# A fused two-block GNN kernel: block 1 projects x that is centred but not yet scaled, and the leaky ReLU moves ahead of the mask

## The chip, the cores and the metric

The kernel runs on one core of one Trainium2 chip. The metric is the device time of one execution in microseconds; times are medians of three runs. The engines are TensorE (PE, matrix products), VectorE (DVE), ScalarE (ACT), GpSimd (POOL) and SyncE (SP, which issues loads). Each works through its own instructions in order and waits on semaphores that the others raise.

## The reference

256 nodes with 768 features, 4096 edges sorted by destination, self-loops added. Two graph attention networks, each behind a residual and a layer norm without gain:

```python
x = layernorm(x + L0(x))     # L0: gat_conv, 8 heads of 768, elu, gat_conv, 1 head of 768
x = layernorm(x + L1(x))     # L1: below; layernorm(v) = (v - mean) / sqrt(var + 1e-5)

# L1, with h0 = its input
h = gat_conv(h0, W1, a_src1, a_dst1, b1)          # 4 heads of 256
h = relu(layer_norm(h) * g1 + be1) + (h0 @ Wr1 + br1)
o = gat_conv(h, W2, a_src2, a_dst2, b2)           # 1 head of 768
out = layer_norm(o) * g2 + be2 + (h @ Wr2 + br2)

# gat_conv, for each head
xl = x @ W
e  = leaky_relu(a_src . xl[src] + a_dst . xl[dst], 0.2)
alpha = exp(e - max over the node's edges) / sum over the node's edges
out[dst] += alpha * xl[src]
```

## The kernel before

Nodes are two tiles of 128 rows (i = 0, 1). The edge list is turned into a dense 256 x 256 matrix of counts, so that a softmax over a node's edges is one over a row, with `far` (-1e30) where there is no edge. Every product is made in three passes, with each operand split into a rounded high part and a low part: ACT rounds (`..._hi`), POOL or DVE subtracts (`..._lo`), PE sums hi x hi, hi x lo and lo x hi. Nothing is scheduled by a tool: each engine's order is written out by hand.

**Weights.** SP loads them into `raw`, ACT rounds each chunk of 128 rows (`split_hi`, in block 1 `chunks_hi`, L373), POOL subtracts it (`split_lo`, in block 1 `chunks_lo`, L380), PE takes it when POOL's count says so. In block 1 there are 24 chunks of 128x512, numbered in this order: W1's first half (0 to 5, `w1a`), its second half (6 to 11, `w1b`), Wr1's halves (12 to 17 and 18 to 23), then 16 chunks of 128x768 for W2 and Wr2. Nine slots of a ring hold the wide chunks, so the rounding of chunk 9 and later ones waits until PE has used chunk 0 and later ones for tile 1. PE's order in block 1 is: transposes of x, w1a for tile 0, w1a for tile 1, w1b for tile 0 (with the scores of heads 0 and 1 ahead of chunk 8), w1b for tile 1, Wr1.

**Block 0** (`A_CONV2` is the index of its second convolution) takes one head per turn of a loop. A head's chain is: dot products of the features with both attention vectors (DVE, L1402), the source dots spread over all columns by PE (`scores`, L968), masking with a running maximum (`masked_scores`, L1457, DVE), four operations of 2 to 4 columns that make two biases, two exponentials per tile on ACT (L746 and L747, since exp of a leaky ReLU is the larger of two exponentials), DVE's maximum of the two and product with the counts (L1477 and L1481, or L1509 and L1511), then the transposes of the weights and PE's aggregation.

**Between the blocks** DVE adds x to the convolution's result (`y_piece`, L1655), takes mean and variance (`y_stats`), POOL takes the inverse root (`inverse_root`, L629 and L632), DVE applies both (`x1`, L1666), PE transposes (`transpose_x1`, L1186), ACT rounds, DVE subtracts, PE projects (`wide_product`, L1202). Dummy products (`keep_warm`, L934) fill PE's gaps. POOL's part of this stretch is

```python
chunks_lo(wide[:6])
for i in range(NT):
    inverse_root(0, i)
chunks_lo(wide[6:9])

pool.wait_ge(rows_loaded, 16 * 8)
pool.tensor_tensor(rows_d[:, 2, :], rows_d[:, 2, :], rows_d[:, 3, :], ALU.add).then_inc(be_added, 1)
pool.wait_ge(be_added, 1)
pool.wait_ge(x1_done, NT)
for i in range(NT):
    pool.tensor_tensor(shift(i), x_sb[:, i, :], rows_d[:, 2, :], ALU.add).then_inc(shifted, 1)
chunks_lo(wide[9:])
```

with the two additions L651 and L655. `shift` is x plus constants, wanted only for the output.

**In block 1** the bias of the residual product is laid into PSUM by PE ahead of it (`residual_bias`, L1217).

Of the kernel before, what the change touches and what calls it, by code (L numbers as in the profile page):

```python
# [117 lines left out]
def build_gnn(nc, x, src, dst, b0_W1, b0_as1, b0_ad1, b0_b1, b0_W2, b0_as2, b0_ad2, b0_b2,  # L118
# [5 lines left out]
    with ctx:  # L124
# [42 lines left out]
        cap1 = sb("cap1", [P, PAIRS])  # L167
        cap2 = sb("cap2", [P, PAIRS])
        bias1 = sb("bias1", [P, PAIRS])
        bias2 = sb("bias2", [P, PAIRS])  # L170
# [6 lines left out]
        rstd = sb("rstd", [P, NT])  # L177
        partial = sb("partial", [P, 2])
# [29 lines left out]
        NAT_AT = [6 * BANK, 0]  # L208
# [3 lines left out]
        TOP1_AT = 7 * BANK  # L212
        X1T_AT = [3 * BANK, 5 * BANK]
# [4 lines left out]
        TOP_AT = T_AT + N  # L218
# [46 lines left out]
        cap_done = sem("cap_done")  # L265
        e_done = sem("e_done")
        e_max_done = sem("e_max_done")
# [7 lines left out]
        bias_done = sem("bias_done")  # L275
# [35 lines left out]
        x1_done = sem("x1_done")  # L311
        tile0_done = sem("tile0_done")
# [145 lines left out]
        def tops(a):  # L458
            at = TOP1_AT + 2 * first_head(a) if is_gat1(a) else ACC if a is FIRST_HEAD else TOP_AT
            return ps[:, at:at + NT * heads_of(a)]  # L460

        def small(a):
            return slice(2 * first_head(a), 2 * (first_head(a) + heads_of(a)))

# [3 lines left out]
        def x1T_part(t, i, part):  # L468

            k0, k1 = 0 if part == 0 else X1T_PARTS[0], X1T_PARTS[part]  # L470
            at = X1T_AT[i] + k0 * P
            return (t[:, k0:k1, i * P:(i + 1) * P],
                    ps[:, at:at + (k1 - k0) * P].rearrange("p (k n) -> p k n", n=P))
# [19 lines left out]
        ON_ACT = [(3, 0)]  # L493

# [92 lines left out]
        def _(pool):  # L587
# [35 lines left out]
            def inverse_root(n, i):  # L623
# [8 lines left out]
                pool.tensor_tensor(rstd[:, i:i + 1], ve[:, i:i + 1], half[:, :], ALU.pow).then_inc(rstd_done, 1)  # L632
# [33 lines left out]
        def _(act):  # L666
# [56 lines left out]
            def features_hi(a, tiles=range(NT)):  # L723
                for i in tiles:
                    if a == A_GAT2:
                        act.wait_ge(b2_added, i + 1)
                    else:
                        act.wait_ge(a_dst_done, before(a) + HH * (i + 1))
                    act.activation(feat(h_hi, a, i), source_at(a, i), ACT.Copy).then_inc(h_hi_done, 1)
# [8 lines left out]

            def exps(a, order):

                act.wait_ge(bias_done, 2 * a + 2)
                for i in order:
                    for k in range(first_head(a), first_head(a) + heads_of(a)):
                        c = 2 * k + i
                        at = masked_at(a, k - first_head(a), i)
                        act.activation(e1[:, k, i, :], at, ACT.Exp, bias=bias1[:, c:c + 1]).then_inc(e_done, 1)  # L746
                        act.activation(at, at, ACT.Exp, bias=bias2[:, c:c + 1], scale=SLOPE).then_inc(e_done, 1)  # L747
# [44 lines left out]
            def softmax_and_elu(h, last=False):  # L792
                projected_hi(h)
# [23 lines left out]
            projected_hi(0)  # L817
            att_for(1)

            act.wait_ge(counted, NT)  # L820
            act.activation(ramp_sum, ps[:, COUNT_AT[0]:COUNT_AT[0] + NT * N], ACT.Copy).then_inc(ramps_copied, 1)
            for c in (0, 1, 2):
                split_hi(act, 2, c)
            exps(0, (1, 0))
            split_hi(act, 2, 3)
# [25 lines left out]
            act.wait_ge(a_dst_done, before(A_CONV2) + 2)  # L851
# [5 lines left out]
            chunks_hi(3, 9)  # L857
            for i in range(NT):
# [15 lines left out]
            for half_at, v in ((0, b1_as2), (1, b1_ad2)):  # L874
                act.dma_start(att[:, half_at * D:(half_at + 1) * D], v[0:1, :].partition_broadcast(P))\
                   .then_inc(att_loaded, 16)
            exps(A_GAT1B, (0, 1))
            chunks_hi(21, 24)
            weights_hi(A_GAT1B)
            chunks_hi(24, 27)  # L880

# [4 lines left out]
            h1_hi(0, 0)  # L886
            chunks_hi(27, 30)
# [7 lines left out]
            chunks_hi(36, 39)  # L895
            features_hi(A_GAT2, tiles=(1,))
# [6 lines left out]
        def _(pe):  # L903
# [205 lines left out]
            for c in range(CH):  # L1109
                if c == 2:  # L1110
                    pe.wait_ge(b1_ready, 2)
                    count_edges(0, COUNT_HALF)
                    count_loops()
                    count_edges(COUNT_HALF, ET)
                if c == 3:
                    scores(0)
# [74 lines left out]
            keep_warm(4, idle)  # L1191

            def wide_product(q, at, i, biased=False, passes=ALL):
# [4 lines left out]
                for n, (a, b) in enumerate(three(node_tile(xT_hi, k, i), node_tile(xT_lo, k, i),  # L1198
# [3 lines left out]
                    last = pe.matmul(ps[:, to:to + HW], a, b, start=k == 0 and n == 0 and not biased,  # L1202
# [5 lines left out]
            def residual_bias(part):  # L1208

                if part == 0:  # L1210
                    pe.wait_ge(pick_set, 3)
                    pe.wait_ge(bias_row_done, 2)
                else:
                    pe.wait_ge(bias_done, 2 * A_GAT1B + 2)
                for i in range(NT):
                    to = 4 * BANK + i * HC + part * HW
                    pe.matmul(ps[:, to:to + HW], bias_pick[0:BIAS_ROWS, :], bias_rows[part],  # L1217
                              start=True, stop=False, skip_group_check=True)
# [22 lines left out]
            transpose_x1(1)  # L1241
            for i in range(NT):
                for q in w1a[2:] if i == 0 else w1a:
                    if q["k"] == X1T_PARTS[0] or i == 1 and q["k"] == 0:
# [27 lines left out]
            residual_bias(0)  # L1272
            for i in range(NT):
                for q in wr1a:
# [6 lines left out]
                    last = wide_product(q, 4 * BANK, i, biased=True)  # L1281
                if i == 0:
                    last.then_inc(r_done, 1)
# [10 lines left out]
            residual_bias(1)  # L1294
            for i in range(NT):
                for q in wr1b:
                    if i == 0 and q["k"] == 3:
                        aggregate_half(A_GAT1B)
                    if i == 1 and q["k"] == 2:
                        transpose_h1(0, 0)  # L1300
                    last = wide_product(q, 4 * BANK, i, biased=True)
                if i == 0:
                    last.then_inc(r_done, 1)
# [5 lines left out]
            for q in w2[:H1_PART]:  # L1309
                if q["k"] == 2:  # L1310
                    transpose_h1(0, 1)
                w2_product(q, 0)
# [34 lines left out]
        def _(dve):  # L1347
# [42 lines left out]

            def dots(a, t, half_at, done, tiles=range(NT)):
# [4 lines left out]
                for i in tiles:  # L1396
# [3 lines left out]
                    for k in range(first_head(a), first_head(a) + n):  # L1400
# [4 lines left out]
                                                 1.0 - SLOPE if half_at else 1.0, 0.0,  # L1405
# [40 lines left out]
            def masked_scores(a):  # L1446

                n = heads_of(a)
                top = tops(a)
                if not in_block0(a):  # L1450
                    dve.wait_ge(scores_bc, a + 1)
                if is_gat1(a):
                    dve.wait_ge(h_lo1_done, 2 * late(a) + 2)
                for k in range(n):
                    for i in range(NT):
                        at = s_at(a, k)
                        dve.tensor_tensor_reduce(masked_at(a, k, i), ps[:, at:at + N], far[:, i, :], 1.0, -3.0e38,  # L1457
                                                 ALU.add, ALU.max, top[:, 2 * k + i:2 * k + i + 1])\
                           .then_inc(masked, 1)
                upto = before(a) + 2 * n  # L1460
                dve.wait_ge(masked, upto)
                dve.wait_ge(a_dst_done, upto)
                d, of = a_d[:, small(a)], small(a)
# [415 lines left out]
```

## Time and profile before

| | |
|---|---|
| median of 3 runs (lowest, highest) | 373.2 us (372.81, 374.55) |
| the profiled execution's own time | 373.22 us |
| its span, first to last instruction | 371.1 us |
| mean granted TensorE clock | 0.998 of full speed |
| busy: PE, PE's weight loads, DVE, ACT, POOL | 355.4, 304.1, 219.4, 213.7, 247.6 us |

The profile is one execution. A row of a timeline gives start, duration, engine, line, operation, output and inputs, shapes, and how many equal instructions are merged; in brackets how long the engine had been idle and what ended it. Starts are counted from the span's start. The ends of matrix products are modelled, so their starts are the better mark: a product of 512 columns starts every 0.228 us.

### The profile page before, as it was taken

To read this page: it belongs to the slowest core of one execution; us is meant where nothing else is said; L and a number is where in the kernel's file an instruction comes from. 1 tells how busy PE (TensorE), PEld (TensorE's weight loads), DVE (VectorE), ACT (ScalarE), POOL (GpSimd) and SP (SyncE) were. 2 spreads that over 40 slices of the span, in tenths; PEclk is the share of its full clock that TensorE was granted. 3 is DMA by queue.
4 is the path that set the end of the run, shared out by engine and by line. 5 is a ranking of instruction groups with operands and counts; after the bars stand their busy time and mean duration, and the time that the engine had idled before them with its cause. 6 is when DMAs were issued, how large, how long until landed. Compare 5 with 4: busy or idle time off the path is not lost.

```text
span 371.1 us, 6198 instructions
## 1 busy us (share of the span) xinstructions
PE 355.4 (96%) x2104; PEld 304.1 (82%) x2104; DVE 219.4 (59%) x570; ACT 213.7 (58%) x373; POOL 247.6 (67%) x170
## 2 busy tenths in 40 slices
PE   7899979999999999999999999998988999999994
PEld 4788868888988988898898898897666788888883
DVE  3996766428328345543741923736776788763875
ACT  4996466756755664673765665565352667244601
POOL 2789619595866947849668595692268976397911
PEclk9999999999999999999999999999999999999999
DMA  7979936637637536754663752755073256436002
GB/s 250 320 244 262 389 128 197 224 95 250 178 96 257 184 134 180 241 172 126 215 239 98 251 174 91 241 188 204 0 219 134 90 165 193 165 94 242 8 0 85
DMA packets 24544, 65.15 MB, mean 176 GB/s; under 512 B 1952, under 2 KB 3024, under 8 KB 24528
## 3 DMA queue, kind: packets, MB, share of 16 engines
q1 hardware_dynamic: 20720, 55.19, 44.7%
q10 hardware_dynamic: 3808, 9.76, 8.8%
q8 instruction: 9, 0.15, 0.2%
q14 instruction: 7, 0.06, 0.0%
HBM read 64.15 MB, written 0.79 MB: 175 GB/s over the span
## 4 chain that ended last, share of the span: by engine, by line
PE 71%; ACT 7%; DVE 6%; issue 6%; POOL 5%; DMA 4%; SPq 0%; POOLq 0%; DVEq 0%; ACTq 0%
PE ps L918 52%; PE ps L1202 7%; PE ps L1003 6%; DMA raw<-in_L_gnn_W 4%; POOL ring_lo L364 3%; ACT ring_hi L351 2%; PE ps L982 1%; PE ps L1268 1%; PE ps L1036 1%; ACT rows_hc L689 1%; POOL ring_lo L380 1%; ACT z L689 1%; PE ps L968 1%; ACT am L689 1%; POOL x_sb L619 1%
## 5 line engine op out<-in xcount | busy, mean ns | idle before, releaser
L364 POOL TENSOR_TENSOR ring_lo<-raw,ring_hi 128x768 fp32r<-128x768 f32 x94 | 170.7, 1851 | 75.1 <-ACT ring_hi L351 75.0
L351 ACT ACTIVATE ring_hi<-raw 128x768 fp32r<-128x768 f32 x96 | 77.5, 851 | 35.2 <-PE ps L918 28.6
L380 POOL TENSOR_TENSOR ring_lo<-raw,ring_hi 128x512 fp32r<-128x512 f32 (+1 forms) x40 | 59.7, 1521 | 24.0 <-ACT ring_hi L373 23.9
L1402 DVE CUSTOM_DVE_ANT_0 e<-ps,att 128x768 f32<-128x768 f32 (+1 forms) x54 | 40.0, 796 | 51.3 <-PE ps L918 48.7
L918 PE MATMUL ps<-ring_hi,zT_hi 128*128 128x512 f32 (+1 forms) x256 | 69.4, 346 | 0.9 <-DVE zT_lo L1558 0.6
L918 PE MATMUL ps<-ring_lo,zT_hi 128*128 128x512 f32 (+1 forms) x256 | 67.4, 338 | 0.0
L918 PE MATMUL ps<-ring_hi,zT_lo 128*128 128x512 f32 (+1 forms) x256 | 67.2, 338 | 0.0
L918 PE MATMUL ps<-ring_hi,xT_hi 128*128 128x512 f32 x192 | 51.3, 343 | 2.3 <-POOL ring_lo L364 1.0
L918 PE MATMUL ps<-ring_lo,xT_hi 128*128 128x512 f32 x192 | 50.3, 339 | 0.0
L918 PE MATMUL ps<-ring_hi,xT_lo 128*128 128x512 f32 x192 | 50.2, 338 | 0.0
L918 PEld LDWEIGHTS ps<-ring_hi,zT_lo 128*128 128x128 f32 x256 | 43.2, 188 | 5.6
L918 PEld LDWEIGHTS ps<-ring_lo,zT_hi 128*128 128x128 f32 x256 | 43.1, 188 | 5.6
L918 PEld LDWEIGHTS ps<-ring_hi,zT_hi 128*128 128x128 f32 x256 | 42.0, 189 | 6.6 <-DVE zT_lo L1558 0.9
L1549 DVE SCALAR_TENSOR_TENSOR ps<-ps,b_plus,z 128x256 f32<-128x256 f32 x48 | 21.2, 487 | 29.2 <-ACT z L776 29.2
L918 PEld LDWEIGHTS ps<-ring_hi,xT_hi 128*128 128x128 f32 x192 | 32.3, 188 | 7.4 <-issue 1.5
L373 ACT ACTIVATE ring_hi<-raw 128x512 fp32r<-128x512 f32 (+1 forms) x40 | 26.6, 722 | 17.9 <-PE ps L918 10.0
L918 PEld LDWEIGHTS ps<-ring_hi,xT_lo 128*128 128x128 f32 x192 | 32.8, 188 | 4.2
L918 PEld LDWEIGHTS ps<-ring_lo,xT_hi 128*128 128x128 f32 x192 | 32.8, 188 | 4.1
L721 ACT ACTIVATE h_hi<-ps 128x768 fp32r<-128x768 f32 x18 | 13.7, 809 | 22.4 <-DVE a_d L1402 20.8
L1003 PE MATMUL ps<-pT_hi,h_hi 128*128 128x256 f32 x96 | 26.2, 284 | 0.3 <-ACT pT_hi L753 0.3
L1003 PE MATMUL ps<-pT_hi,h_lo 128*128 128x256 f32 x96 | 26.1, 283 | 0.0
L1558 DVE SCALAR_TENSOR_TENSOR zT_lo<-ps,zT_hi 128x512 fp32r<-128x512 f32 x24 | 16.6, 692 | 15.9 <-ACT zT_hi L782 15.9
(163 smaller groups left out, 562.2 us busy)
## 6 DMA issues: line engine op xcount, KB each, us to landing
raw<-in_L_gnn_W SPq DMA_DIRECT2D x54, 768.0 KB, 4.4
raw<-in_L_gnn_Wr SPq DMA_DIRECT2D x8, 768.0 KB, 4.3
att<-in_L_gnn_a_src ACTq DMA_DIRECT2D x10, 384.0 KB, 4.6
att<-in_L_gnn_a_dst ACTq DMA_DIRECT2D x10, 384.0 KB, 5.4
raw<-in_L_gnn_W SPq DMA_DIRECT2D x4, 384.0 KB, 6.1
x_sb<-in_x SPq DMA_DIRECT2D x3, 256.0 KB, 5.7
rows_hc<-in_L_gnn_b SPq DMA_DIRECT2D x1, 512.0 KB, 6.3
rows_hc<-in_L_gnn_g SPq DMA_DIRECT2D x1, 512.0 KB, 7.2
```

The lines of the kernel that those rows point to most:

```text
L351: eng.activation(slot_hi(c), raw_chunk(c), ACT.Copy).then_inc(hi_done, 1)
L364: eng.tensor_tensor(slot_lo(c), raw_chunk(c), slot_hi(c).bitcast(F32), ALU.subtract)\
L373: eng.activation(ring_hi[:, q["ring_at"]:q["ring_at"] + w], raw[:, q["raw_group"], q["raw_at"]:q["raw_at"] + w], ACT.Copy)\
L380: eng.tensor_tensor(ring_lo[:, q["ring_at"]:q["ring_at"] + w], raw[:, q["raw_group"], q["raw_at"]:q["raw_at"] + w], ring_hi[:, q["ring_at" ...
L689: act.activation(ramp(t), iota[:, :], ACT.Relu, bias=bias).then_inc(ramp_act_done, 1)
L721: act.activation(feat(h_hi, h, i), source_at(h, i), ACT.Copy).then_inc(h_hi_done, 1)
L918: last = pe.matmul(ps[:, at + to:at + to + hi - lo], a, b[:, lo:hi], start=start and n == 0 and to != D, stop=stop and n == PASSES - 1, sk ...
L1003: return pe.matmul(ps[:, at:at + N], feat(features, 0, j)[:, ch:ch + P], weights_part[:, 0, j, :], start=first, stop=final, skip_group_che ...
L1202: last = pe.matmul(ps[:, to:to + HW], a, b, start=k == 0 and n == 0 and not biased, stop=k == KD - 1 and n == PASSES - 1, skip_group_check ...
L1402: dve.tensor_tensor_reduce(junk[:, at:at + w], of[:, (k - first_head(a)) * w:(k - first_head(a) + 1) * w], att[:, half_at * row + k * w:ha ...
L1549: dve.scalar_tensor_tensor(ps[:, at:at + N], ps[:, at:at + N], b1_plus[:, bass.ds(KD * h + t, 1)], z[:, t * N:(t + 1) * N], ALU.add, ALU.m ...
L1558: dve.scalar_tensor_tensor(zT_lo[:, 2 * q:2 * q + 2, :].rearrange("p k n -> p (k n)"), ps[:, at:at + 2 * N], -1.0, hi.bitcast(F32), ALU.ad ...
```

## The change

It has two parts.

1. In every softmax the leaky ReLU is formed first. ACT forms 0.2 x (source dot) - 0.8 x (destination dot) (`leaks`, the destination dots now come multiplied by -0.8), DVE takes the maximum with the source dot (`leaky_scores`), then masks it, negated, with a running minimum (`tile_tops`), and ACT takes one exponential with that minimum as its bias. The four small operations and the second exponential go. In block 0's heads the low part of the features of one tile stands on each side of `tile_tops`.
2. Between the blocks, x is centred in PSUM's and ACT's passes with a mean from running sums, and goes to the transposes without the root. The root is taken meanwhile and put on the dot products, on the features (`scale` of ACT's rounding, one factor in DVE's subtraction) and, by four new ACT passes (`residual_scale`), on Wr1's product, behind which the bias is now added. x itself is scaled by ACT (`x1_scale`), which raises `x1_done`. The ten dummy products behind the aggregation go, and two stay of four behind the transposes.

POOL's code is not touched but for the root's name. The core of the diff:

```diff
+            def leaks(a):
+
+                act.wait_ge(scores_bc, a + 1)
+                for i in range(NT):
+                    act.wait_ge(a_dst_done, before(a) + heads_of(a) * (i + 1))
+                    for k in range(heads_of(a)):
+                        at = s_at(a, k)
+                        act.activation(e1[:, first_head(a) + k, i, :], ps[:, at:at + N], ACT.Identity,
+                                       bias=a_d[:, pair(a, k, i)], scale=SLOPE).then_inc(leak_done, 1)
...
+                for n, i in enumerate(order):
+                    act.wait_ge(masked, before(a) + heads_of(a) * (n + 1))
+                    for k in range(heads_of(a)):
+                        at = masked_at(a, k, i)
+                        act.activation(at, at, ACT.Exp, bias=top[:, pair(a, k, i)], scale=-1.0).then_inc(e_done, 1)
...
             def softmax_and_elu(h, last=False):
+                leaks(h)
                 projected_hi(h)
                 exps(h, (1, 0))
...
-            act.wait_ge(a_dst_done, before(A_CONV2) + 2)
+            leaks(A_CONV2)
             projected_tile_hi(A_CONV2, 1)
...
-            chunks_hi(3, 9)
-            for i in range(NT):
...
+            def centre_wide(i):
+
+                lo, hi = NAT_PIECES[0]
+                act.wait_ge(mean_done, i + 1)
+                act.activation(x_sb[:, i, lo:hi], ps[:, NAT_AT[i] + lo:NAT_AT[i] + hi], ACT.Identity,
+                               bias=minus_mean[:, i:i + 1]).then_inc(wide_centred, 1)
...
+            def x1_scale(i):
+
+                act.wait_ge(x1T_ps, 2 * i + 2)
+                act.wait_ge(rstd_done, i + 1)
+                act.activation(x_sb[:, i, :], x_sb[:, i, :], ACT.Copy, scale=rstd0[:, i:i + 1]).then_inc(x1_done, 1)
+
+            def residual_scale(part, i):
+
+                if i == 0:
+                    act.wait_ge(r_product, part + 1)
+                else:
+                    act.wait_ge(chunk_used, plan[(3 + part) * KD - 1]["n"] + 1)
+                of = ps[:, 4 * BANK + i * HC + part * HW:4 * BANK + i * HC + (part + 1) * HW]
+                act.activation(of, of, ACT.Copy, scale=rstd0[:, i:i + 1]).then_inc(r_scaled, 1)
+
+            chunks_hi(3, 6)
+            centre_wide(0)
+            chunks_hi(6, 7)
+            x1_hi(0)
+            centre_wide(1)
+            chunks_hi(7, 9)
+            x1_hi(1)
+            x1_scale(0)
+
             features_hi(A_GAT1A, tiles=(0,))
             chunks_hi(9, 14)
+            x1_scale(1)
             features_hi(A_GAT1A, tiles=(1,))
             chunks_hi(14, 15)
+            leaks(A_GAT1A)
             exps(A_GAT1A, (0, 1))
...
-            idle = WT_AT[0]
-            keep_warm(10, idle)
 
             def transpose_x1(i):
 
-                pe.wait_ge(x1_done, i + 1)
+                pe.wait_ge(wide_centred, i + 1)
                 for k in range(KD):
-                    at = X1T_AT[i] + k * P
+                    if k == X1T_PARTS[0]:
+                        pe.wait_ge(rest_centred, i + 1)
...
             transpose_x1(0)
-            keep_warm(4, idle)
...
+            keep_warm(2, PROJ)
...
+                    if i == 0 and q["k"] == 5:
+                        residual_bias(0, 0)
+                        residual_bias(0, 1)
...
             def softmax(h):
-                masked_scores(h)
-                projected_lo(h)
+                leaky_scores(h)
+                dve.wait_ge(leaky_done, 2 * h + 2)
+                projected_lo(h, 0)
+                for i in (1, 0):
+                    tile_tops(h, i)
+                projected_lo(h, 1)
                 normalised(h)
                 weights_lo(h)
...
             y_piece(0, 0)
             y_piece(0, 1)
-            y_stats(0)
+            y_centre(0)
             y_piece(1, 0)
-            x1(0)
             y_piece(1, 1)
-            y_stats(1)
+            y_centre(1)
             x1_lo(0, 0)
             x1_lo(0, 1)
-            x1(1)
+            y_stats(0)
+            y_stats(1)
             x1_lo(1, 0)
             x1_lo(1, 1)
```

How the instructions stand on the engines. On PE, from the dummies behind the aggregation to the first projection's second pair of chunks, before (`x_sb` is x, `ring` the weights, `xT` the transposed x):

```order
L934 MATMUL ps<-zeros 128x512 x10
L1186 MATMUL ps<-ident,x_sb 128x128 [waits x1_done]
L1186 MATMUL ps<-ident,x_sb 128x128 x5
L934 MATMUL ps<-zeros 128x512 x4
L1202 MATMUL ps<-ring_hi,xT_hi 128x512 [waits lo_pool,x1T_hi_done]
...
L1202 MATMUL ps<-ring_hi,xT_lo 128x512 [waits lo_pool]
L1186 MATMUL ps<-ident,x_sb 128x128 [waits x1_done]
L1186 MATMUL ps<-ident,x_sb 128x128 x5
```

and now:

```order
L1245 MATMUL ps<-ident,x_sb 128x128 [waits wide_centred]
L1245 MATMUL ps<-ident,x_sb 128x128 x3
L1245 MATMUL ps<-ident,x_sb 128x128 [waits rest_centred]
L1245 MATMUL ps<-ident,x_sb 128x128
L994 MATMUL ps<-zeros 128x512 x2
L1261 MATMUL ps<-ring_hi,xT_hi 128x512 [waits lo_pool,x1T_hi_done]
```

The ten dummies are gone and the transposes wait for the centring. Those of tile 1 now stand four chunks into the projection, where two stood before.

On ACT, from the rounding of tile 1's transposes to the features of tile 1, before (`h_hi` are block 1's features):

```order
L861 ACTIVATE xT_hi<-ps 128x2x128 [waits x1T_ps]
L729 ACTIVATE h_hi<-ps 128x512 [waits a_dst_done]
L373 ACTIVATE ring_hi<-raw 128x512 [waits chunk_used,raw_full0]
L373 ACTIVATE ring_hi<-raw 128x512 [waits chunk_used] x2
L373 ACTIVATE ring_hi<-raw 128x512 [waits chunk_used,raw_full1]
L373 ACTIVATE ring_hi<-raw 128x512 [waits chunk_used]
L729 ACTIVATE h_hi<-ps 128x512 [waits a_dst_done]
```

and now:

```order
L889 ACTIVATE xT_hi<-ps 128x2x128 [waits x1T_ps]
L895 ACTIVATE x_sb<-x_sb,rstd 128x768 [waits rstd_done,x1T_ps]
L737 ACTIVATE h_hi<-ps,rstd 128x512 [waits a_dst_done]
L378 ACTIVATE ring_hi<-raw 128x512 [waits chunk_used,raw_full0]
L378 ACTIVATE ring_hi<-raw 128x512 [waits chunk_used] x2
L378 ACTIVATE ring_hi<-raw 128x512 [waits chunk_used,raw_full1]
L378 ACTIVATE ring_hi<-raw 128x512 [waits chunk_used]
L895 ACTIVATE x_sb<-x_sb,rstd 128x768 [waits rstd_done,x1T_ps]
L737 ACTIVATE h_hi<-ps,rstd 128x512 [waits a_dst_done]
```

The scaling of x is new on ACT: tile 0's ahead of the first features, tile 1's behind the five chunks that follow them.

On POOL the rows of this stretch stand as before, now with these lines:

```order
L385 TENSOR_TENSOR ring_lo<-raw,ring_hi 128x512 [waits hi_done] x3
L658 TENSOR_TENSOR rows_d<-rows_d 128x768 [waits rows_loaded]
L662 TENSOR_TENSOR am<-x_sb,rows_d 128x768 [waits x1_done,be_added]
L662 TENSOR_TENSOR am<-x_sb,rows_d 128x768
L385 TENSOR_TENSOR ring_lo<-raw,ring_hi 128x512 [waits hi_done] x15
```

Nothing moved here; `x1_done` is raised by ACT's L895 and no longer by DVE.

## Rows read from the trace of the kernel before

**Rows 1.** The page, part 1: engine, busy us, share of the span, instructions.

```profile
PE 355.4 (96%) x2104; PEld 304.1 (82%) x2104; DVE 219.4 (59%) x570; ACT 213.7 (58%) x373; POOL 247.6 (67%) x170
```

**Rows 2.** The list of waits, PE: us in total, times, longest.

```profile
PE ps L1186 <- DVE x_sb L1666: 1.0, 1, 1.0
...
PE ps L1290 <- DVE z L1735: 0.2, 1, 0.2
```

**Rows 3.** The timeline, PE, from the aggregation to w1a's last product for tile 0.

```profile
275.39 2.33 PE L934 MATMUL ps<-zeros 128*128 128x512 bf16 x10
277.73 0.87 PE L1186 MATMUL ps<-ident,x_sb 128*128 128x128 f32 x6
...
279.12 0.58 PE L1202 MATMUL ps<-ring_hi,xT_hi 128*128 128x512 f32 x1
...
281.86 0.88 PE L1186 MATMUL ps<-ident,x_sb 128*128 128x128 f32 x6 [1.00 <-DVE x_sb L1666]
...
285.09 0.39 PE L1202 MATMUL ps<-ring_hi,xT_lo 128*128 128x512 f32 x1
```

**Rows 4.** The timeline, POOL and DVE's second x1, 280 to 298.

```profile
280.11 4.08 POOL L380 TENSOR_TENSOR ring_lo<-raw,ring_hi 128x512 fp32r<-128x512 f32 x3
280.18 1.63 DVE L1666 TENSOR_SCALAR x_sb<-z,mv,rstd 128x768 f32<-128x768 f32 x1
...
284.15 1.84 POOL L651 TENSOR_TENSOR rows_d<-rows_d 128x768 f32<-128x768 f32 x1
...
286.07 3.66 POOL L655 TENSOR_TENSOR am<-x_sb,rows_d 128x768 f32<-128x768 f32 x2
...
289.68 7.57 POOL L380 TENSOR_TENSOR ring_lo<-raw,ring_hi 128x512 fp32r<-128x512 f32 x6
```

**Rows 5.** The timeline, PE's weight load ahead of w1b's chunk 11, tile 0.

```profile
293.54 0.19 PEld L1202 LDWEIGHTS ps<-ring_hi,xT_hi 128*128 128x128 f32 x1 [0.47 <-POOL ring_lo L380]
```

**Rows 6.** The timeline of one head of block 0's loop, all engines.

```profile
207.31 1.51 ACT L721 ACTIVATE h_hi<-ps 128x768 fp32r<-128x768 f32 x2 [2.79 <-DVE a_d L1402]
...
212.63 0.88 DVE L1516 TENSOR_SCALAR am<-ps,rz 128x256 f32<-128x256 f32 x2
...
214.28 0.60 PE L982 MATMUL ps<-ident,am 128*128 128x128 f32 x4
```

**Rows 7.** The timeline of A_CONV2's softmax, all engines.

```profile
266.97 0.43 DVE L1457 CUSTOM_DVE_ANT_0 ps<-ps,far 128x256 f32<-128x256 f32 x1 [0.18 <-PE ps L968]
...
268.31 0.47 ACT L746 ACTIVATE e<-ps,bias 128x256 f32<-128x256 f32 x1 [0.68 <-DVE bias L1468]
...
268.68 0.44 ACT L747 ACTIVATE ps<-ps,bias 128x256 f32<-128x256 f32 x1
...
269.62 0.42 DVE L1481 SCALAR_TENSOR_TENSOR e<-ps,counts 128x256 f32<-128x256 f32 x1
...
270.11 0.44 PE L994 MATMUL ps<-ident,e 128*128 128x128 f32 x2 [0.59 <-DVE e L1481]
...
271.12 0.48 PE L1036 MATMUL ps<-h_hi,pT_hi 128*128 128x512 f32 x1
```

**Rows 8.** The timeline, DVE's first dots of block 1 and ACT behind them.

```profile
285.63 0.42 DVE L1402 CUSTOM_DVE_ANT_0 e<-ps,att 128x256 f32<-128x256 f32 x1 [1.43 <-PE ps L1202]
...
287.13 0.60 ACT L729 ACTIVATE h_hi<-ps 128x512 fp32r<-128x512 f32 x1 [3.71 <-DVE a_d L1402]
...
287.63 2.71 ACT L373 ACTIVATE ring_hi<-raw 128x512 fp32r<-128x512 f32 x5
```

**Rows 9.** Groups by line and shape, ACT: busy us, mean ns, idle before.

```profile
L351 ACT ACTIVATE ring_hi<-raw 128x768 fp32r<-128x768 f32 x96 | 77.5, 851 | 35.2 <-PE ps L918 28.6 <-DMA raw<-in_L_gnn_W 6.6
...
L734 ACT ACTIVATE x_sb<-z,offset,rstd 128x768 f32<-128x768 f32 x1 | 1.0, 1028 | 12.6 <-POOL offset L635 12.6
```

**Rows 10.** The timeline, PE, the bias products ahead of Wr1's first half.

```profile
298.56 0.73 PE L1217 MATMUL ps<-zT_hi,bias_pick 33*128 33x512 f32 x2
```

**Rows 11.** The timeline, PE, the dummies at the kernel's start.

```profile
1.34 3.58 PE L934 MATMUL ps<-zeros 128*128 128x512 bf16 x8 [1.34 <-POOL zeros L589]
```

More of the change, by code:

```diff
@@ L886, in _ @@
             h1_hi(0, 0)
+            residual_scale(1, 1)
             chunks_hi(27, 30)
@@ L1201, in wide_product @@
                         continue
-                    last = pe.matmul(ps[:, to:to + HW], a, b, start=k == 0 and n == 0 and not biased,
+                    last = pe.matmul(ps[:, to:to + HW], a, b, start=k == 0 and n == 0,
                                      stop=k == KD - 1 and n == PASSES - 1, skip_group_check=True)
@@ L1206, in wide_product, with residual_bias @@
                 return last
[L1208 to L1218, printed above, removed]
+            def residual_bias(part, i):
+                pe.wait_ge(pick_set, 3)
+                pe.wait_ge(bias_row_done, 2)
+                pe.wait_ge(r_scaled, R_ORDER.index((part, i)) + 1)
+                to = 4 * BANK + i * HC + part * HW
+                pe.matmul(ps[:, to:to + HW], bias_pick[0:BIAS_ROWS, :], bias_rows[part],
+                          start=False, stop=True, skip_group_check=True).then_inc(r_done, 1)
             def narrow_product(q, at, i, tile, **more):
@@ new lines, in leaky_scores, with tile_tops @@
+                dve.wait_ge(leak_done, before(a) + NT * n)
+                for i in range(NT):
+                    for k in range(n):
+                        at = s_at(a, k)
+                        dve.tensor_tensor(masked_at(a, k, i), ps[:, at:at + N], e1[:, first_head(a) + k, i, :], ALU.max)\
+                           .then_inc(leaky_done, 1)
+            def tile_tops(a, i):
+                n = heads_of(a)
+                for k in range(n):
+                    if isinstance(a, int):
+                        dve.wait_ge(leaky_done, before(a) + n * i + k + 1)
+                    at = masked_at(a, k, i)
+                    dve.tensor_tensor_reduce(at, at, far[:, i, :], -1.0, 3.0e38, ALU.add, ALU.min, top[:, pair(a, k, i)])\
+                       .then_inc(masked, 1)
@@ L1478, in weigh @@
-                for k in range(n):
-                    c = 2 * (g + k) + i
-                    dve.wait_ge(e_max_done, before(a) + n * i + k + 1)
-                    dve.scalar_tensor_tensor(e2[:, g + k, i, :], masked_at(a, k, i), 1.0, counts[:, i, :],
-                                             ALU.mult, ALU.mult, accum_out=zsum[:, c:c + 1]).then_inc(p_done, 1)
-            def dots0(h):
-                dve.wait_ge(att_loaded, 32 * (h + 1))
-                dots(h, a_s, 0, a_src_done)
-                dots(h, a_d, 1, a_dst_done, tiles=(0,))
-                dve.wait_ge(scores_bc, h + 1)
-                dots(h, a_d, 1, a_dst_done, tiles=(1,))
@@ L1562, in _ @@
             both_dots(0)
-            projected_lo(0)
+            for i in range(NT):
+                projected_lo(0, i)
+            dve.wait_ge(h_lo0_done, NT)
+            leaky_scores(0)
             bank = ps[:, COUNT_AT[0]:COUNT_AT[0] + NT * N].rearrange("p (i n) -> p i n", n=N)
@@ L1642, in _ @@
             inverse_sums(A_CONV2)
-            y = [z[:, i * D:(i + 1) * D] for i in range(NT)]
             dve.wait_ge(xb_done, NT)
@@ L1804, in _ @@
                .then_inc(eps_done, 1)
+            y = [z[:, i * D:(i + 1) * D] for i in range(NT)]
             nat = [ps[:, GAT2_NAT_AT[i]:GAT2_NAT_AT[i] + D] for i in range(NT)]
```

188 lines of the change are left out of this document (98 added, 90 removed).

## The prediction

> **What bounds the kernel now.** I read the page first: TensorE (PE) is busy for 355.4 us, 96% of the span [rows 1], so only work or waits that stand in PE's own stream can move the end. Then the list of waits: all of PE's together are small, and the one that the change aims at, the wait of the transposes (L1186) for the normalised x (L1666), is 1.0 us [rows 2]. Then PE's timeline between the aggregation of block 0's second convolution and block 1's first projection: ten dummy products fill 275.39 to 277.73, six transposes of x's tile 0 follow, four more dummies, the first projection at 279.12, and the transposes of tile 1 wait until 281.86; the last product of the first projection's tile 0 starts at 285.09 [rows 3]. The dummies count as busy but do nothing, so some 3 to 4 us of this stretch could be saved. Last, GpSimd's timeline (POOL) of the same stretch [rows 4] and PE's row at 293.54 [rows 5]: three chunks of W1's second half are subtracted on POOL behind the two additions L655, and PE waits for the last of them. POOL delivers chunk 11 at 289.68 + 3 x 1.26 = 293.46 and PE takes it at 293.54. Here POOL, not PE, sets the time.
>
> **The new softmax.** In every softmax two exponentials per tile, two maxima behind them and four small operations become two ScalarE (ACT) reads, two maxima ahead of the masking, and one exponential per tile. In block 0's heads PE never waits for it. Before, the last of VectorE's (DVE) normalising ends at 212.63 + 0.88 = 213.51 and PE transposes at 214.28, a slack of 0.77 [rows 6]. After: the last dot product ends just ahead of ACT's start at 207.31 [rows 6], so the second ACT read runs from 207.33 to 207.80, maxima 207.83, h_hi done 209.20, h_lo tile 0 from 209.23 (0.87 to the next), two maskings of 0.35, h_lo tile 1, two products with the counts, sums and normalising: end 213.64. The slack is 0.64: cost 0 in the six heads of the loop, for as long as this cover holds; beyond it each 0.1 us costs 0.6 in all. Heads 0 and 1 lose nothing that lasts.
>
> At A_CONV2 the chain is bare. Before: DVE masks PE's scores at 266.97, its product with the counts starts at 269.62 for tile 0, PE's transposes at 270.11, the aggregation at 271.12 [rows 7]. After, DVE first waits for two ACT reads (0.37 from start to start, 0.47 long, as the exponentials in [rows 7]), to 267.83, then runs one maximum more ahead of the weights and the four small operations (0.5) less: the product of tile 0 starts at 270.10 instead of 269.62, tile 1 is where it was, and ACT's copy lets the aggregation start 0.35 later. **Term 1: +0.35.**
>
> **The shorter front.** The transposes of tile 0 wait for centred x, not for the root. DVE's sum and mean end near 274.6, ACT's centring (0.6) near 275.25; PE is through with the aggregation at 275.39 + 0.35 = 275.74, so they start there instead of at 277.73. From them to the first projection it is 1.39 as before (277.13); then 1.12 + 0.46 for the two chunks, 1.37 for two more, 0.63 for tile 1's transposes, which find their data centred by 277.9, and 1.22 up to the last product's start: 281.93 for the former 285.09. **Term 2 (with term 1 inside): PE is 3.16 early** at this point. Bounds: 2.6 if mean and centring take 0.5 longer, 3.5 if the softmax costs nothing.
>
> **What is late next.** POOL's order is untouched: chunks 0 to 5, two roots, chunks 6 to 8, the addition L651, a wait for both tiles of normalised x, the two L655 (3.61 from start to end), and only then chunk 9 [rows 4]. But x is now normalised by ACT (x1_scale), and the one of tile 1 stands behind features_hi of tile 0 and behind five chunks. Before, DVE met the wait at 280.18 + 1.63 = 281.81 and POOL came to it at 286.07 [rows 4]. After:
> - the roots: DVE's statistics now stand behind tile 0's low parts, tile 1's are ready at 280.6, the root takes 0.9 more, and chunk 6 starts at 281.47 instead of 280.11; with the 5.96 from there to L655 POOL reaches the wait at 287.4;
> - DVE's dots start 0.54 after PE's last product, as before (285.09 to 285.63): 282.47; ACT's features start 1.50 later, the five chunks 0.50 after that and last 2.71 with the last start 0.1 earlier than their end [rows 8]: to 287.2. the last of them, chunk 13, must also wait until PE has used W1's fifth chunk for tile 1, at 282.16 + 15 x 0.228 and some 0.3 for the result to land, 285.9, which it has;
> - x1_scale of tile 1: a 768-wide ACT pass is 0.85 plain and 1.03 with two operands per partition [rows 9]; with one I take 0.93: done near 288.2.
> So L655 starts at 288.2 instead of 286.07, chunk 9 is there at 291.8 + 1.26 = 293.1, chunk 11 at 295.6. PE wants chunk 9 at 281.93 + 0.23 + 27 x 0.228 + 0.44 = 288.75 and stands for 4.3 us. It takes chunk 11 at 295.65 for the former 293.54. **Term 3: all of term 2 is gone, and PE is 2.1 late.** How early PE came to the stall doesn't matter; only ACT's chain does. Bounds: L655 can't start before W1's fifth chunk is used for tile 1 (285.9), one ACT chunk (0.54) and the scaling (0.85) later, 287.3, which makes it 1.2 late; if each link of ACT's chain takes 0.1 to 0.2 more it is 2.9.
>
> **Behind it.** Four bias products move: two pairs in front of Wr1's halves (0.73 a pair [rows 10]) become one pair and two singles, with a change of operands around each; the trace shows no single one, so between 0 (the same work) and 0.7 (a pair's 0.73 for each single), and I take the nearer end, 0.2. The waits that they bring (for four ACT scalings of Wr1's product) are met: by ACT's order each scaling is done before PE comes to its bias product, the third by only some 0.3. PE's wait of 0.25 for DVE at L1290 [rows 2] is filled by them: -0.2. No wait of PE for block 1's scores or weights is in the list before, and PE now comes later to them; the last softmax loses its four small operations and gains the read, and PE's wide products cover it. **Term 4: 0** (-0.2 to +0.5).
>
> **Sum.** 2.1 + 0 on the profiled execution's own 373.22 us (371.1 of span and 2.1 around it), which is the median of the three runs, 373.2: **375.3 us**, 0.56% slower. About 0.5% (1.87 us, so beyond 375.07 or 371.33) is what a measurement of this kernel tells from no change.
>
> **Rivals.**
> 1. *The stall also costs the clock* (28%). PE has nothing to do for 4.3 us at 288.75 and is half idle until 295.65. In this trace PE never stands so long after the start: dummies fill such gaps, and the granted clock stays at its upper level, 2.4 GHz (0.998 in the mean). What half of it costs shows at the start: there eight dummies take 3.58 us (0.448 each) [rows 11], and ten take 2.33 (0.233) in [rows 3]. At half speed chunks 9 to 11 take 1.3 each and end 0.6 later, and what is left of some 3.6 us of slow running falls on tile 1's products: 0.6 to 2.1 more, 1.3 as the middle: **376.6**. Against it: 4.3 us may be too short for the clock to fall. The Trainium skill, TensorE: Matmul & The Clock Gate, "HAM oscillation", says that an array left idle between bursts goes back to the lower clock and begins the next burst cold; by that, this rival would be the forecast. No stretch of this trace shows such a wait, so it stays a rival.
> 2. *Less is lost* (10%). If ACT's chain runs ahead and L655 starts at 287.3 (the lower bound), PE is 1.2 late: **374.4**, not to be told from no change.
> 3. *The front's gain survives* (6%): the other side. It needs POOL to deliver chunk 9 before PE asks for it, so L655 to begin before 283.8, or POOL to be quick enough to catch up. It then ends at 373.2 - 3.2 + 0.2 = **370.2**. It decides at an L655 start of 284.2: earlier is faster by 0.5%, and at 286.07 there is no change. For it speaks that PE really has the 3.16; against it that POOL itself can't be at L655 before 285.3 and that x1_scale stands where it stands.
> 4. *The heads lose their cover* (6%). If ACT's two reads come 0.2 later than the 0.64 of slack allows, six heads lose 1.2: 376.5.
>
> **Chances.** My forecast (POOL late by 1.6 to 2.6, clock kept: 374.8 to 376.0, of which 60% lie above 375.07) has 50%. Slower by over 0.5%: 0.30 + 0.27 (rival 1) + 0.06 (rival 4) = 0.63. Within 0.5%: 0.20 + 0.01 + 0.09 = 0.30; the rest of rival 2 and rival 3 make faster 0.07. The range: rivals 1 and 4 reach to 377.4, rival 2's upper half to 374.1; what lies below holds about 0.12, above 0.06.
>
> **What would show it.** In the trace of after: PE's transposes of x at about 275.7 with no wait before tile 1's; the last product of tile 0 at 281.9; L655's successor on POOL starting at 288.2 with a wait for ACT's scaling ahead; a wait of PE for POOL of about 4.3 us, the longest of all, near 289, and two of 0.6 behind it; chunk 11 used at 295.65; the heads of block 0 with PE's period unchanged. The granted clock behind 293 tells forecast from rival 1. I'd be wrong if the scaling on ACT came before the five chunks in time, if POOL's wait were met by 286, or if block 0's heads grew.

## The result, and the profile after

The changed kernel takes 377.5 us in the median of 9 runs (376.03 to 378.76), the kernel before in 9 runs beside it 372.81 us (372.23 to 374.55): a ratio of 1.0123, 95% interval 1.010 to 1.0146. It is slower, as forecast (375.3), and 0.1 us above the range (374.1 to 377.4). A second set of 6 runs gave 377.5 again.

The profiled execution took 378.57 us, with a span of 376.7 us, 5.6 us more than the kernel before. Some 2 us of these arise in the first 11 us, where TensorE's rate differs from run to run in either kernel (last section). The heads of block 0, whose softmax is new, add nothing: from the start-up's 16 products with `am` (26.06 in the kernel before, 28.05 here) to PE's scores of block 0's second convolution it is 240.46 us there and 240.40 here. So positions are compared behind these scores, a mark that all kernels have. They start at 266.52 in the kernel before and at 268.45 here, 1.93 later, each behind the same wait of 0.68. **From this mark to the end of the span the kernel before takes 104.58 us and the changed one 108.25: 3.67 more.** "On before's scale" below means 1.93 less. Of the kernel before, the timeline, PE, has the mark and the last product of w1b:

```profile
266.52 0.40 PE L968 MATMUL ps<-ident,a_s 128*128 128x128 f32 x2 [0.68 <-DVE a_s L1624]
...
298.23 0.40 PE L1202 MATMUL ps<-ring_hi,xT_lo 128*128 128x512 f32 x1
```

The page of the changed kernel, parts 1 and 2, against [rows 1]: PE is busy longer for fewer instructions, and the row of the granted clock has one slice at 6.

```profile
PE 357.5 (95%) x2092; PEld 306.0 (81%) x2092; DVE 213.3 (57%) x529; ACT 221.0 (59%) x382; POOL 247.3 (66%) x170
...
PEclk9999999999999999999999999999999699999999
```

The list of waits of the changed kernel, PE (us in total, times, longest), against [rows 2]: the wait for normalised x and the 0.2 us at the transposes of h1 are gone, and one of 4.3 us for POOL is there.

```profile
PE ps L1261 <- POOL ring_lo L385: 4.3, 1, 4.3
```

The timeline of the changed kernel, PE, from the second convolution to the end of the slow stretch, against [rows 3]:

```profile
268.45 0.40 PE L1028 MATMUL ps<-ident,a_s 128*128 128x128 f32 x2 [0.68 <-DVE a_s L1683]
...
273.51 0.47 PE L1096 MATMUL ps<-h_hi,pT_hi 128*128 128x512 f32 x1 [0.22 <-ACT pT_hi L775]
...
277.77 0.82 PE L1245 MATMUL ps<-ident,x_sb 128*128 128x128 f32 x6
278.43 0.59 PE L994 MATMUL ps<-zeros 128*128 128x512 bf16 x2
279.06 0.50 PE L1261 MATMUL ps<-ring_hi,xT_hi 128*128 128x512 f32 x1
...
283.77 0.40 PE L1261 MATMUL ps<-ring_hi,xT_lo 128*128 128x512 f32 x1
...
290.50 0.39 PE L1261 MATMUL ps<-ring_hi,xT_lo 128*128 128x512 f32 x1
295.19 0.79 PE L1261 MATMUL ps<-ring_hi,xT_hi 128*128 128x512 f32 x1 [4.31 <-POOL ring_lo L385]
295.79 0.63 PE L1261 MATMUL ps<-ring_lo,xT_hi 128*128 128x512 f32 x1
296.21 0.63 PE L1261 MATMUL ps<-ring_hi,xT_lo 128*128 128x512 f32 x1
...
300.48 0.44 PE L1261 MATMUL ps<-ring_hi,xT_hi 128*128 128x512 f32 x1
300.75 0.39 PE L1261 MATMUL ps<-ring_lo,xT_hi 128*128 128x512 f32 x1
```

The rows show the front shortened to 283.77 (tile 0's last product of w1a), the stall ahead of chunk 9, and behind it products 0.43 us apart instead of 0.23 up to 300.48. What releases the stall stands in the timeline of the changed kernel, POOL and ACT, against [rows 4]:

```profile
286.67 2.70 ACT L378 ACTIVATE ring_hi<-raw 128x512 fp32r<-128x512 f32 x5
...
287.16 1.86 POOL L658 TENSOR_TENSOR rows_d<-rows_d 128x768 f32<-128x768 f32 x1
...
289.27 0.93 ACT L895 ACTIVATE x_sb<-x_sb,rstd 128x768 f32<-128x768 f32 x1
...
290.34 3.57 POOL L662 TENSOR_TENSOR am<-x_sb,rows_d 128x768 f32<-128x768 f32 x2 [1.32 <-ACT x_sb L895]
...
293.87 7.45 POOL L385 TENSOR_TENSOR ring_lo<-raw,ring_hi 128x512 fp32r<-128x512 f32 x6
```

POOL waits 1.32 us for `x1_scale` of tile 1 (L895), adds for 3.6 us, and only then subtracts chunk 9. The stretches of the changed kernel (length, busy times of PE, PEld, DVE, ACT and POOL with their instructions, granted clock, DMA share, GB/s): the clock leaves its upper level (1.00, 2.4 GHz) between 293 and 295, when PE has had nothing to do since 290.9, and is at the lower one (0.50, 1.2 GHz) until past 299.

```profile
291.00:293.00 2.00, 0.00 (x0) 0.00 (x0) 0.73 (x1) 1.93 (x5) 2.00 (x2) 1.00 0.06 21
293.00:295.00 2.00, 0.00 (x0) 0.00 (x0) 1.97 (x7) 0.00 (x0) 2.00 (x2) 0.68 0.00 0
295.00:297.00 2.00, 1.81 (x4) 1.38 (x5) 0.99 (x6) 1.58 (x4) 2.00 (x3) 0.50 0.00 0
297.00:299.00 2.00, 2.00 (x6) 1.47 (x5) 0.00 (x0) 0.00 (x0) 2.00 (x3) 0.50 0.20 17
299.00:301.00 2.00, 2.00 (x7) 1.52 (x7) 1.45 (x7) 0.00 (x0) 2.00 (x2) 0.61 0.86 324
```

### The profile page after: what moved, and what is told of

Read it like the earlier page. It is cut to its first block, busy times and chain, and to the rows that moved or that the text cites. A ratio compares the mean times of both kernels' runs of the same rounds, so it can differ in the third digit from the quotient of the medians.

```text
span 376.7 us, 6149 instructions
## 1 busy us (share of the span) xinstructions
PE 357.5 (95%) x2092; PEld 306.0 (81%) x2092; DVE 213.3 (57%) x529; ACT 221.0 (59%) x382; POOL 247.3 (66%) x170
## 4 chain that ended last, share of the span: by engine, by line
PE 85%; DVE 6%; ACT 5%; POOL 2%; issue 1%; POOLq 0%; DVEq 0%; ACTq 0%
PE ps L978 59%; PE ps L1261 8%; PE ps L1063 7%; PE ps L1096 2%; PE ps L1155 2%; PE ps L1325 2%; PE ps L1042 2%; DVE e L1470 1%; PE ps L994 1%; DVE ps L1607 1%; POOL am L662 1%; PE ps L1028 1%; ACT zT_hi L798 1%; ACT ring_hi L356 1%; PE ps L1120 1%
## 5 line engine op out<-in xcount | busy, mean ns | idle before, releaser
L1470 DVE CUSTOM_DVE_ANT_0 e<-ps,att 128x768 f32<-128x768 f32 x38 | 34.2, 954 | 48.8 <-PE ps L978 48.8
L978 PE MATMUL ps<-ring_hi,xT_hi 128*128 128x512 f32 x192 | 51.9, 346 | 1.9 <-POOL ring_lo L369 1.2
L1261 PE MATMUL ps<-ring_hi,xT_hi 128*128 128x512 f32 x48 | 20.9, 436 | 4.3 <-POOL ring_lo L385 4.3
```

The costliest lines, as they stand in the source:

```text
L978: last = pe.matmul(ps[:, at + to:at + to + hi - lo], a, b[:, lo:hi], start=start and n == 0 and to != D, stop=stop and n == PASSES - 1, sk ...
L1470: dve.tensor_tensor_reduce(junk[:, at:at + w], of[:, (k - first_head(a)) * w:(k - first_head(a) + 1) * w], att[:, half_at * row + k * w:ha ...
```

## The experiments

Theory A: POOL's two additions, late behind ACT's scaling, make the stall, and PE, standing in it, loses its clock. Rivals: B, the early front finds some other engine late, so that the time is lost without the additions too; C, the slow products cost nothing, since POOL's chunks 10 and 11 set the pace there, or they have another cause.

All kernels side by side. "Mark to end" is the profiled span less the start of PE's scores of the second convolution. The changed kernel and that of the seventh experiment, each profiled twice, differ from themselves by 0.09 and 0.02 us; spans are read to 0.1 us, so a difference of 0.1 us means nothing. A ratio is to the kernel before on the same chip.

| kernel | mark to end, us | median, us | of before, us | ratio (95%) |
|---|---|---|---|---|
| before | 371.1 - 266.52 = 104.58 | | | |
| changed | 376.7 - 268.45 = 108.25 | 377.5 | 372.81 | 1.0123 (1.010 to 1.0146) |
| changed, again | 375.0 - 266.66 = 108.34 | 377.53 | 373.65 | 1.0104 (1.0075 to 1.0133) |
| 1 additions later | 370.7 - 266.90 = 103.80 | 372.46 | 373.25 | 0.9985 (0.9963 to 1.0007) |
| 2 scaling earlier | 376.4 - 269.71 = 106.69 | 376.03 | 373.25 | 1.0053 (1.0029 to 1.0076) |
| 3 dummies in the stall | 375.6 - 268.69 = 106.91 | 376.39 | 373.25 | 1.0067 (1.004 to 1.0094) |
| 4 before, additions later | 373.7 - 269.51 = 104.19 | 372.88 | 373.25 | 0.998 (0.9957 to 1.0002) |
| 5 softmax alone | 373.7 - 268.77 = 104.93 | 373.76 | 373.0 | 1.0019 (1.0003 to 1.0036) |
| 6 additions later, order | 370.3 - 267.07 = 103.23 | 372.06 | 373.0 | 0.9974 (0.996 to 0.9988) |
| 7 front alone, additions later | 369.2 - 266.75 = 102.45 | 370.8 | 373.65 | 0.9923 (0.9898 to 0.9949) |
| 7 again | 370.3 - 267.83 = 102.47 | 370.66 | 373.08 | 0.9939 (0.992 to 0.9958) |
| 8 front alone, order | 369.3 - 266.51 = 102.79 | 371.15 | 373.08 | 0.9945 (0.9922 to 0.9967) |

**1. The additions behind the W1 and Wr1 chunks.**

```diff
 chunks_lo(wide[6:9])
+chunks_lo(wide[9:18])
 pool.wait_ge(rows_loaded, 16 * 8)
 pool.tensor_tensor(rows_d[:, 2, :], rows_d[:, 2, :], rows_d[:, 3, :], ALU.add).then_inc(be_added, 1)
+chunks_lo(wide[18:21])
 pool.wait_ge(be_added, 1)
...
-chunks_lo(wide[9:])
+chunks_lo(wide[21:])
```

> The changed kernel with GpSimd's additions behind the last W1 chunks: rows_d's addition after wide chunk 17, the two additions of the shift after wide chunk 20; all else as in the changed kernel. Theory A (the stall is made by the wait of these two additions for ScalarE's scaling, and their 3.6 us): chunk 9 is subtracted from 287.2 on, 3.7 us after chunk 8 or less, PE's wait of 4.3 us is gone, the granted clock stays at its upper level, and Wr1's first product starts some 7 us earlier than in the changed kernel: 369.5 to 370.3 us. Rival B (the front is late for another reason, so that the next link, ScalarE's chunks or VectorE's dots and softmax, takes the stall over): a wait of 1 to 4 us stands at the same place or at the first weights, 371.5 to 374 us.

It takes 4.45 us less from the mark on (108.25 to 103.80); its median of 372.46 us is 2.2 to 3.0 us longer than A had it. PE's products of w1b run without a wait and the granted clock is 1.00 in every stretch from 283 to 301, so A is right about the stall. But the front isn't worth what was put on it: two new waits of PE for the softmax weights take 2.1 us of its lead, as B says. The timeline of this kernel, PE and DVE:

```profile
291.46 1.43 DVE L1525 TENSOR_TENSOR ps<-ps,e 128x256 f32<-128x256 f32 x4 [1.30 <-ACT e L756]
...
298.24 1.09 PE L1044 MATMUL ps<-ident,e 128*128 128x128 f32 x8 [1.35 <-DVE e L1548]
...
310.47 1.09 PE L1044 MATMUL ps<-ident,e 128*128 128x128 f32 x8 [0.76 <-DVE e L1548]
```

Ahead of the first, DVE waits 1.30 us for ACT's new reads before it can take the maxima. That this wait makes the one of PE is not shown: experiment 7, without these reads, keeps 1.25 of the 1.35 us.

**2. The scaling ahead of the five chunks.**

```diff
-            chunks_hi(9, 14)
             x1_scale(1)
+            chunks_hi(9, 14)
```

> The changed kernel with ScalarE's scaling of x's tile 1 ahead of the five chunks 9 to 13 instead of behind them. Theory A: GpSimd no longer waits for it and begins the additions 1.3 us earlier, at 289.0 on the changed kernel's time scale; PE's wait shrinks from 4.3 to 3.0 us. If the clock falls all the same: 375.2 us. If 3.0 us are too short for that: 373.8 us. Rival B (the chunks behind the scaling on ScalarE are what GpSimd waits for next, 0.9 us later each): no gain, 376.5 us.

PE's wait for chunk 9 is 3.11 us instead of 4.31. The clock falls all the same, but later and for less long (windows, this kernel): it is at its upper level when PE begins again at 295.26, and PE's products are slow only from 296.50 to 299.6. The gain is 1.56 us, where theory A had 1.3 for the case that the clock falls all the same. 1.19 of it is the earlier end of the stall (295.26 - 269.71 = 25.55 us behind the mark for 295.19 - 268.45 = 26.74). The 0.37 left fit the shorter slow stretch.

```profile
295.00:297.00 2.00, 1.47 (x4) 0.98 (x5) 2.00 (x10) 0.48 (x2) 2.00 (x3) 0.82 0.00 0
297.00:299.00 2.00, 2.00 (x6) 1.41 (x6) 0.25 (x2) 1.09 (x3) 2.00 (x3) 0.50 0.07 24
299.00:301.00 2.00, 2.00 (x9) 1.59 (x8) 1.42 (x7) 0.00 (x0) 2.00 (x2) 0.83 0.82 283
```

**3. Dummies in the stall.**

```diff
+                    if i == 0 and q["k"] == 3:
+                        keep_warm(18, 4 * BANK)
                     last = wide_product(q, 0, i)
```

> The changed kernel with 18 dummy products (0.23 us each, 4.2 us) in the stall, into a bank that nobody uses, just ahead of chunk 9. Theory A (the idle engine loses its clock): PE resumes at the same time, 295.2, the granted clock stays at its upper level, and Wr1's first product comes 1.4 us earlier: 375.1 us where the changed kernel without its slower start has 376.5. Rival C (the clock falls for another reason, or the slow products were hidden behind GpSimd's chunks 10 and 11): no change, 376.5 us.

1.34 us less from the mark on, where A had 1.4, and the granted clock is 1.00 in every stretch from 283 to 303. PE gets each chunk as POOL has it (timeline, this kernel):

```profile
290.97 4.06 PE L994 MATMUL ps<-zeros 128*128 128x512 bf16 x18
295.47 0.50 PE L1261 MATMUL ps<-ring_hi,xT_hi 128*128 128x512 f32 x1 [0.44 <-POOL ring_lo L385]
...
296.71 0.50 PE L1261 MATMUL ps<-ring_hi,xT_hi 128*128 128x512 f32 x1 [0.28 <-POOL ring_lo L385]
...
297.94 0.50 PE L1261 MATMUL ps<-ring_hi,xT_hi 128*128 128x512 f32 x1 [0.27 <-POOL ring_lo L385]
```

Chunk 9 is taken 26.78 us behind the mark, 26.74 in the changed kernel. C falls: nothing but PE's idleness differs, and 1.34 us is what the clock cost.

**4. The kernel before with the same move of the additions** (the diff of 1).

> The kernel before with the same move of GpSimd's additions. Theory A: the kernel before loses only the 0.2 us in front of chunk 11: 372.7 us, no change to be measured. Rival: the additions behind chunk 20 delay later chunks, some tenths of a us more, 373.3 us.

0.39 us less by the profile. The wait ahead of chunk 11 is gone: PE is at the bias products ahead of Wr1 31.72 us behind the mark (301.23) for 32.04 (298.56), 0.32 earlier. The wait of 0.25 us at the transposes of h1 [rows 2] is still there (list of waits of this kernel, PE), and the last 0.1 us, no more than the rounding of the spans, stays unexplained.

```profile
PE ps L1292 <- DVE z L1737: 0.3, 1, 0.3
```

By the timed runs no change is shown (0.9957 to 1.0002). So the 4.45 us of experiment 1 belong to the changed order, not to the additions as such.

**5. The new softmax alone** in the kernel before (its diff is the change's, without what concerns x's scaling).

> The kernel before with the new softmax alone (ScalarE's reads, maxima ahead of the masking, one exponential, the counts copied by ScalarE in head 0); the normalised x, the 14 dummies and the bias products stay as before. My working: the heads lose nothing, the chain at the second convolution is 0.46 us longer as in the changed kernel's trace, and PE's wait for chunk 11 (0.2 us) hides half of nothing, since GpSimd moves along: 373.2 us or 0.1 to 0.2% over the kernel before. Rival: the heads lose 0.1 each or more, 0.6 us on top: 373.9 us.

0.35 us more from the mark on, and 0.19% by the timed runs. From the 16 products with `am` of the start-up (26.06 in the kernel before, 28.32 here) to the mark it is 240.46 and 240.45: the heads lose nothing.

**6. More order on top of 1.** ACT: `leaks` of 1A ahead of chunk 14, `x1_scale(1)` behind the exponentials, `leaks` of 1B ahead of chunks 18 to 20 (the move of the additions stays as in 1). DVE:

```diff
             weigh(A_GAT1A, 0)
-            half_lo(A_GAT1B, 0)
             weigh(A_GAT1A, 1)
+            half_lo(A_GAT1B, 0)
```

> The changed kernel with GpSimd's additions moved as in the first experiment, and with three moves for the waits for weights (1.35 and 0.76 us) that stood in its trace: ScalarE reads the leaks of 1A ahead of chunk 14 and scales x's tile 1 behind the exponentials of 1A; it reads the leaks of 1B ahead of chunks 18 to 20; VectorE multiplies both tiles of 1A with the counts ahead of the low part of 1B's tile 0. If those two waits stood for themselves: 2.1 us less than the first experiment, 370.3 us where that has 372.4. Rival: VectorE is full there (19 us of work in 20), and the waits come back at the scores of 1B or at its aggregation: 371 to 372.4 us.

Both waits are gone and 0.57 of 2.1 us is gained; the list of waits of this kernel has a new one, at the first transposes of h1.

```profile
PE ps L1348 <- DVE z L1804: 1.0, 1, 1.0
```

The rival is right in the main, though the wait came back one step later than it said: these transposes start 53.26 us behind the mark (320.33) for 53.85 in 1 (320.75). DVE's chain to h1 ends little earlier, wherever PE waits for it.

**7. The front alone:** the change without its softmax, the additions as in 1.

> The centred front and the moved bias products without the new softmax, with GpSimd's additions moved as in the first experiment: that experiment's kernel with the softmax of before. If the new softmax costs only its 0.46 us at the second convolution: 371.9 us where the first experiment has 372.4. If it also makes the waits for weights that stood there (1.35 and 0.76 us), because VectorE now waits for ScalarE's reads ahead of the maxima: 370.5 us or less. If the old softmax is the longer one for VectorE in block 1, as its four maxima and four small operations behind the exponentials may make it: 372.4 us or more.

The second case comes close: 1.35 us less than experiment 1. 0.48 of it is the second convolution (scores to aggregation 4.58 us here, 271.96 - 266.90 = 5.06 in 1), 0.86 the waits for weights (1.25 here, 2.1 there): the first of the two, 1.35 in 1, is nearly all there with the softmax of before, so it comes with the front; the second, 0.76, is gone. This is the best kernel of the study, 0.6 to 0.8% faster than the kernel before.

**8. Order on top of 7:** the DVE move of 6, and `x1_scale(1)` behind the exponentials. The kernel of 7 ran beside it once more.

> The previous kernel (centred front, softmax of before, GpSimd's additions behind the W1 chunks) with two moves for the wait of 1.25 us for weights at 297.56 in its trace: ScalarE scales x's tile 1 behind the exponentials of 1A, and VectorE multiplies both tiles of 1A with the counts ahead of the low part of 1B's tile 0. VectorE's last product with the counts then starts near 296.1 instead of 297.1 and the wait is gone or under 0.3 us: 369.6 us where that kernel has 370.6. Rival: as in the kernel with the new softmax, where three such moves took 2.1 us of waits away and brought 0.4, VectorE is late again at the first transposes of h1: 370.2 us.

> The previous kernel once more beside it, nothing edited, for the comparison on the same chip: 370.6 us in its faster group.

The wait of 1.25 us is gone, and one of 0.7 us for DVE at the first transposes of h1 and one of 0.3 us for POOL have come: 0.3 us more than 7, not less. Even the rival was too hopeful. The first transposes of h1 start 52.53 us behind the mark in 7 (319.28) and 52.86 here (319.37).

**9. The changed kernel once more.**

> The changed kernel once more, with nothing edited, to see whether the 2 us by which its runs fall into two groups (376.0 to 376.9 and 377.5 to 378.8) belong to the change. If they come from the start, where the kernel before shows them too (12 of 31 runs between 374.0 and 375.8, 19 between 372.2 and 373.5): the faster group lies at 376.5 again and holds half of the runs or more, and a profile of it has PE's first projection at its full rate. If they belong to the change: its runs stay at 377.5 to 378.8 in most.

From the mark on it takes 108.34 us, and its mark stands at 266.66, as in the kernel before. The stall is 4.3 us again. But its runs are no faster than at first (377.53 us), and only two of the six lie in the faster group, where half or more were expected. So this leaves open whether the 2 us at the start come more often with the change than without it. That they come without it too is shown by experiment 4, whose start is that of the kernel before: its mark stands at 269.51.

## Why the prediction was right, and where it was off

On before's scale:

- **Heads: cost 0**, right. The normalising ends at 215.65, PE transposes at 216.21, 1.93 behind [rows 6]: a slack of 0.56, forecast 0.64. Experiment 5 confirms it.
- **Term 1, +0.35.** The aggregation starts 5.06 us behind the scores for 4.60 (271.12 [rows 7] less the mark): 0.46. Experiment 5 has 0.35 at the end.
- **Term 2, PE 3.16 early.** Transposes at 275.84 (forecast 275.74), first projection at 277.13 (277.13), tile 0's last product at 281.84 (281.93), so 3.25 early. That these agree to 0.1 is in part luck: the aggregation ended 0.1 later than forecast, and the way from the transposes to the first projection, with two dummies for four, took 1.29 for the 1.39 that the forecast kept. No wait ahead of tile 1's transposes.
- **Term 3, the stall,** right in mechanism and size. Chunk 6 at 281.46 (281.47), POOL at the wait at 287.09 (287.4), the additions from 288.41 (288.2), chunk 9 taken at 293.26 (293.1), stall 4.31 (4.3). With the clock kept, as in experiment 3, the start of Wr1's first product, at 303.96, would be 1.34 earlier, 300.69 on before's scale. The kernel before has the last of w1b at 298.23 and would, without its bias pair, go on at 298.46: 2.2 late for the forecast 2.1.
- **The step that failed is the one on the clock.** The forecast held it at its upper level at 50% and gave its fall, rival 1, 28%. It fell (0.50 from 295 to 299), and cost 1.34 us (experiment 3) where rival 1 had 1.3. The reason given against it, that 4.3 us might be too short, had no row behind it; in experiment 2 the clock fell behind a stall of 3.11 us too (0.50 from 297 to 299). The Trainium skill, TensorE: Matmul & The Clock Gate, "HAM oscillation", was cited for the other side: an array idle between bursts goes back to the lower clock. These two runs agree with it.
- **Term 4, 0.** From the mark on it is 3.67 in all, so 2.2 + 1.34 leave 0.1 for the bias products, in exchange for PE's former wait at L1290, which is gone as forecast. No run tried this term by itself.

So mark to end grew by 3.67 where rival 1 had 376.6 - 373.2 = 3.4 and the forecast 2.1. The medians are 4.7 us apart. That the other 1 us is the start's is not shown, but the runs fit it: the mark stands between 266.5 and 269.7 in the twelve profiles, whichever kernel it is, and the fastest runs of the two kernels are 3.8 us apart (376.03 and 372.23). The forecast had no term for the start.

Rival 3, the front's gain survives, was judged by the start of the additions alone. Experiment 1 shows a second condition that it lacked: with POOL out of the way, DVE's weights are 1.35 and 0.76 us late. Its 370.2 us would not have come: 372.46 did. Of its numbers, 285.3 for POOL's earliest arrival has no working; the prediction's own chain gives 287.4, and POOL came at 287.09. The forecast's range to 376.0 is also 0.2 wider than the 2.6 us it names.

## What to carry to other kernels

A front made shorter is worth what the next engines in line can deliver: before the cut, look for what else waits on the step that was moved (here two additions for the output, in a queue that feeds TensorE) and put it where its queue has slack. Weigh a stall of some microseconds on TensorE with its clock: here 4.3 us of standing cost 1.34 more, and 18 dummy products gave it back. A change of two parts is best tried as two: the front alone, with the additions moved, is 0.6 to 0.8% faster than the kernel before, and with the new softmax on top it is 1.35 us slower.

## What the runs showed of the hardware

- **The rate at the start.** All kernels begin with the same eight dummies, 0.448 us each for 0.233 later [rows 11, rows 3], but the rate rises at different times. In the kernel before the products behind them run at full rate from the first row of the transposes (5.08, four in 0.63). In the changed kernel's first profile (timeline, PE) they don't until 10.9, at 0.32 us a product for 0.175 later, though the granted clock reads 1.00 in the windows of that stretch:

```profile
5.01 1.09 PE L1120 MATMUL ps<-ident,x_sb 128*128 128x128 f32 x4
6.79 1.01 PE L978 MATMUL ps<-ring_hi,xT_hi 128*128 128x512 f32 x2 [0.69 <-ACT xT_hi L700]
7.59 0.84 PE L978 MATMUL ps<-ring_lo,xT_hi 128*128 128x512 f32 x2
...
10.92 0.65 PE L1120 MATMUL ps<-ident,x_sb 128*128 128x128 f32 x4
11.33 0.60 PE L978 MATMUL ps<-ring_hi,xT_hi 128*128 128x512 f32 x2
```

  In the second profile of the same kernel they do from 6.91. Why it differs was not tried. So a granted clock of 1.00 in this stretch doesn't say that products run at full rate.
- **The same stall, the fall at different moments.** In the two profiles of the changed kernel PE stops at 290.9 and at 289.1, 22.4 us behind the mark in both. In the first the stretch 293 to 295 is granted 0.68; in the second, 1.8 us earlier throughout, 291 to 293 has 0.88, 293 to 299 has 0.50 and 299 to 301 has 0.91. The total differs by 0.09 us.
- **A scale per partition costs on DVE.** A dot product of 256 columns starts every 0.35 us with a constant (from 285.63 on in the kernel before, the first of them in [rows 8]) and every 0.40 us with a scale per partition (294.29, 294.69 in experiment 1): 0.05 us each, for 16 of them in block 1.
